# Adding the second-choice rows of four token tiles by DMAs with addition instead of by VectorE

## The reference

```python
logits = xf @ gate_w.T
w, idx = jax.lax.top_k(logits, 2)          # two experts for each of 1024 tokens
w = jax.nn.softmax(w, axis=-1)
combine = zeros((T, 32)).at[arange(T)[:, None], idx].add(w)
out = sum over e of combine[:, e:e+1] * (xf @ expert_w[e].T + expert_b[e])
x = x + out.reshape(x.shape)
```

## Time and profile before

| | us |
|---|---|
| three runs | 287.78, 292.65, 293.7 |
| median | 292.65 |
| the profiled execution's own time | 286.06 |
| its span, first to last instruction | 284.2 |
| mean granted TensorE clock over the span | 0.991 |

### The profile page before, as it was taken

How to read it: one execution, slowest core, us unless ns; L and a number is a source line. 1 busy time by engine, 2 the same in 40 slices (tenths; PEclk the granted TensorE clock), 3 DMA queues, 4 the chain that set the end, 5 groups by cost and what they waited for, 6 DMA issues and landing times.

```text
span 284.2 us, 4478 instructions
## 1 busy us (share of the span) xinstructions
PE 269.6 (95%) x1594; PEld 164.5 (58%) x1594; DVE 140.7 (50%) x404; ACT 77.0 (27%) x138; POOL 69.4 (24%) x69
## 2 busy tenths in 40 slices
PE   7978999999999999999999999999999999999970
PEld 3345677678877778878887775433334333333750
DVE  2368766766913341557441445501665311360895
ACT  1465754334211115223321111221001011113100
POOL 0531600000000000005604113457754442222300
PEclk9999999999999999999999999999999999999996
DMA  7999800000000100019008999926999999984955
GB/s 263 403 352 333 274 12 0 3 0 2 0 37 37 39 1 37 2 44 400 2 4 316 392 421 421 390 76 184 378 405 421 419 413 414 425 361 164 415 198 221
DMA packets 19302, 61.68 MB, mean 217 GB/s; under 512 B 4411, under 2 KB 6107, under 8 KB 14928
## 3 DMA queue, kind: packets, MB, share of 16 engines
q1 hardware_dynamic: 14368, 51.03, 46.2%
q0 software_dynamic: 3472, 7.81, 7.6%
q10 hardware_dynamic: 1440, 2.56, 2.4%
HBM read 54.63 MB, written 13.47 MB: 240 GB/s over the span
## 4 chain that ended last, share of the span: by engine, by line
PE 82%; DVE 8%; DMA 6%; ACT 2%; issue 1%; SPq 0%; DVEq 0%; ACTq 0%; POOLq 0%
PE bank L1368 28%; PE bank L1519 22%; PE bank L1555 15%; DVE acc L1226 4%; PE bank L1492 4%; PE bank L1423 3%; DMA xp_first<-in_xp 2%; PE bank L1251 2%; PE bank L1444 2%; DMA r_tab<-res,recs 2%; DVE acc L1231 2%; DMA wbuf<-r_tab 1%; PE bank L1430 1%; PE bank L1313 1%; DVE y0lo L902 1%
## 5 line engine op out<-in xcount | busy, mean ns | idle before, releaser
L1519 PE MATMUL bank<-wbuf,xT 128*32 128x512 f32 (+1 forms) x432 | 74.0, 598 | 0.0
L1555 PE MATMUL bank<-md,hid 128*128 128x512 f32 x176 | 48.2, 414 | 0.0
L635 POOL DMA_INDIRECT slots<-kept,sid x16 | 15.9, 993 | 122.4 <-DVE sid L1008 119.3
L1519 PEld LDWEIGHTS bank<-wbuf,xT 128*32 128x32 f32 (+1 forms) x432 | 19.9, 122 | 37.5 <-issue 36.5
L1555 PEld LDWEIGHTS bank<-md,hid 128*128 128x128 f32 x176 | 31.7, 189 | 8.3 <-issue 2.9
L1044 DVE COPY xT<-bank 128x512 f32<-128x512 f32 x20 | 13.8, 691 | 44.8 <-PE bank L1492 44.7
L1368 PE MATMUL bank<-y0hi,mg 128*128 128x512 f32 x88 | 35.3, 412 | 0.6 <-ACT y0hi L710 0.6
L1368 PE MATMUL bank<-y0hi,mu 128*128 128x512 f32 x88 | 33.7, 396 | 0.7 <-DVE mu L906 0.7
L1368 PE MATMUL bank<-y0lo,mg 128*128 128x512 f32 x88 | 33.7, 394 | 0.2 <-DVE y0lo L902 0.2
L1368 PE MATMUL bank<-y0lo,mu 128*128 128x512 f32 x88 | 33.6, 393 | 0.0
L828 ACT ACTIVATE res<-bank,recs 128x512 f32<-128x512 f32 x20 | 13.7, 687 | 69.1 <-PE bank L1519 69.1
(11 more groups left out here) (196 smaller groups left out, 300.6 us busy)
## 6 DMA issues: line engine op xcount, KB each, us to landing
wbuf<-in_w SPq DMA_DIRECT2D x32, 1024.0 KB, 13.6
r_tab<-in_zero SPq DMA_DIRECT2D x1, 4096.0 KB, 25.3
wbuf<-r_tab SPq DMA_DIRECT2D x8, 512.0 KB, 7.9
acc<-in_x SPq DMA_DIRECT2D x1, 2048.0 KB, 15.1
y_tab<-yv SPq DMA_DIRECT2D x8, 256.0 KB, 5.7
out<-acc ACTq DMA_DIRECT2D x8, 256.0 KB, 2.2
base<-in_base SPq DMA_DIRECT2D x3, 352.0 KB, 7.3
xp_first<-in_xp SPq DMA_DIRECT2D x1, 1040.0 KB, 7.1
```

The costliest lines, as they stand in the source:

```text
L635: pool.indirect_dma_start(out=slots, out_offset=bass.IndirectOffsetOnAxis(ap=sid[:, j, k:k + 1], axis=0), in_=rec[:, j, k], in_offset=None ...
L1519: v = mm(RS[t % 2][p0:p0 + w], xT[x_slot(t)][:, c, p0:p0 + w], wbuf[buffer(r)][:, c], start=(c == 0), stop=(c == DC - 1))
L1555: v = mm(DN[j % 2][:], hid[:, t, part, c], md[:, c], start=(c == 0 and part == 0), stop=(c == HC - 1 and part == 1))
```

## The change

SyncE now loads both rows only for the tiles 0 to 3, and for the tiles 4 to 7 only the first-choice row. Their second-choice rows are added straight to `acc[:, j]` by four DMAs of 256 KB with `accum_op=ALU.add`, issued by GpSimd at the end of its program, after its own loop and after a semaphore (`rows_out`) that SyncE raises when all scatters have landed. VectorE does one addition instead of two for each of the tiles 4 to 7, and before the first of them it waits until all four accumulating DMAs have landed (`second_in` at 64).

```diff
+        rows_out, second_in = sem("rows_out"), sem("second_in")
@@ block.sync
             for b in range(U):
                 static = len(range(b, TD, U))
                 sp.wait_ge(res_out[b], bodies * 16 + 16 * static if 1 <= b <= XU else 16 * static)
+            sp.sem_inc(rows_out, 1)
             for j in range(NT):
-                sp.dma_start(part(j), r_tab_v[:, 2 * j:2 * j + 2]).then_inc(part_in[j], 16)
+                loaded = 2 if j < TPH else 1
+                sp.dma_start(part(j)[:, 0:loaded], r_tab_v[:, 2 * j:2 * j + loaded]).then_inc(part_in[j], 16)
@@ block.gpsimd, at its end
+            pool.wait_ge(acc2_done, NT)
+            pool.wait_ge(rows_out, 1)
+            for j in range(TPH, NT):
+                pool.dma_start(acc[:, j], r_tab_v[:, 2 * j + 1], accum_op=ALU.add).then_inc(second_in, 16)
@@ block.vector
             def add_part(j):
 
                 dve.wait_ge(part_in[j], 16)
-                for k in range(2):
+                if j >= TPH:
+                    dve.wait_ge(second_in, 16 * TPH)
+                for k in range(2 if j < TPH else 1):
                     link(nc.vector.tensor_tensor(acc[:, j], acc[:, j], part(j)[:, k], ALU.add))
```

## The result

The changed kernel took 295.88 us (median of four runs, 293.88 to 296.52) beside 290.21 us (four runs, 287.45 to 293.7) for the kernel before: a ratio of 1.028 with a 95% interval of 1.019 to 1.036. It is slower; whether by more than 2% this interval leaves open. The ratios leave out slow runs, those more than 1.5% above the fastest of the same kernel, while medians and ranges are of all runs. That matters here: the four runs of the kernel before are two near 287.6 and two near 293.2 us. The ratio of 1.028 fits the means 295.54 and 287.6, a difference of 7.9 us; the medians differ by 5.7 us (1.020), and against the two longer runs it would be some 2.4.

The account below looks back on a forecast made before the run. VectorE's chain of additions was taken to bound the kernel's end; start 267.8, fourth issue 271.8 and landing 3.9 gave T = 275.7, 2.1 us past 273.65, so 294.7 us on the median 292.65, range 288.5 to 298.7.

Parts of the forecast that it names:

- T: Time when the fourth accumulating DMA has landed: GpSimd's start, issues and landing, put at 275.7 us.
- What bounds the kernel: At the end, from 263.96 us, VectorE's unbroken chain of 24 additions; four fewer save 2.9 us at most.
- The end moves with T: VectorE's tail of 7.77 us follows the fourth landing, so the end moves by T - 273.65, +2.1 us.
- small remainder of the pace: Unsized correction in VectorE's chain between the 5.7 us wait less 2.9 saved and the +2.1 us.
- the floor for T: End of VectorE's first eight additions, put at 270.0 us; landing earlier gains no more than 2.9 us.
- rival 2: Descriptor making held up by VectorE's additions, so GpSimd's issues begin only at 270.0: +4.2, 296.9 us; chance 0.06.
- GpSimd's start: First accumulating DMA's issue, 0.5 us behind the third low-part subtraction's end at 267.26: 267.8 us.
- The issues: GpSimd's four direct DMAs, 1.32 us apart like its indirect ones; the fourth issued at 271.8 us.
- The landing: Fourth accumulating DMA, issue to landing: 3.3 us as the gathers plus 0.63 for the second read, 3.9 us.
- Rival 1: At the accumulating DMAs: SyncE-like issues and a 2.7 us landing, T 271.8, end moves -1.9 to 290.8 us; chance 0.12.
- Rival 3: Accumulating DMAs land late, 6.8 us, sharing engines with the loads' rest: T 278.6, +4.9, 297.6 us; chance 0.11.
- Rival 4: DMA engines add much slower than they copy, transfers queue, T = 267.8 + 2.7 + 4x; over 2% from x = 2.25; chance 0.17.

Follow-up runs that it names:

- e2_left_out: The changed kernel without its four GpSimd DMAs and VectorE's wait, second rows of tiles 4 to 7 left out: 283.89 us beside 286.95, ratio 0.989 to the kernel before.
- e12_after: The changed kernel again, unchanged, on another chip, against the kernel before: 290.53 us beside 287.01, ratio 1.011, no stall.
- e11_early: The changed kernel with GpSimd's four DMAs ahead of its third subtraction: 290.13 us, ratio 1.011 to the kernel before.
- e7_one: Only tile 7 gets its second-choice rows by an accumulating DMA, with its own count: 290.46 us beside 291.18 for the kernel before, ratio 0.996.
- e8_after: The changed kernel again, unchanged, on another chip, against the kernel before: 294.1 us beside 291.18, ratio 1.012, with a milder stall.
- e4_before: The kernel before, unchanged, profiled as a control against runs of itself: 286.92 us, ratio 1.001, no stall.
- e6_two: Only tiles 6 and 7 get their second-choice rows by accumulating DMAs, each with its own count: 290.11 us beside 291.18 for the kernel before, ratio 0.993.
- e5_hot_first: The changed kernel with a count per DMA and VectorE's work not touching tiles 4 to 7 of the accumulator first: runs split, 286.82 to 294.37 us.
- e3_each: The changed kernel with a count of its own for each of the four accumulating DMAs: 287.02 us beside 286.95 for the kernel before, ratio 1.000.
- e9_paired: The changed kernel with a count per DMA and each late tile's part and hot sum added together: 285.37 us beside 287.01 for the kernel before, ratio 0.994.

## Why the predicted time was met and the terms behind it were not

**The time: in part luck.** Forecast were +2.1 us on a median of 292.65, 294.7 in all. Measured were 295.88, but beside 290.21 for the kernel before, so +5.7 us. The forecast's time lies within 1.2 us because it started 2.4 us too high. Against the cost without the stall, about 3 us, the forecast of 2.1 is short by 1, and that it isn't short by more is luck too: see T.

**What bounds the kernel: right.** VectorE's chain at the end was the place. Without the second rows (e2_left_out) the time fell by 3.1 us, where 2.9 was worked out.

**The end moves with T: right.** VectorE went idle behind its first eight additions, the accumulating DMA released it, and the tail behind T was 7.77 us in the profile after, as worked out. One row was misread beside it. The addition at 270.02 in the earlier trace rows is the eighth, not the ninth (at 0.73 us of pace the starts from 270.02 to 272.93 are five, the eighth to the twelfth), so the first eight end at 270.7 and the forecast's own T means a wait of 5.0 us, not 5.7. The "small remainder of the pace" is this 0.7 us: 5.0 - 2.9 = 2.1. The time doesn't suffer, as it was worked out from T - 273.65; the floor for T and the start of the issues in rival 2 belong at 270.7 as well.

**T: 1.2 us too early, by three errors that partly cancel.** Counted from VectorE's first part addition, so that executions compare, the prediction put T at 275.7 - 263.96 = 11.7 us, and the execution without the stall had 12.9. The terms:
- GpSimd's start was put 0.5 us behind the subtraction. It was at once (267.29 + 1.74 = 269.03, and the first issue is drawn from 268.97; in other profiles 0.1 to 0.2 us lie between). Counted from VectorE's first addition the start was due at 3.8 us and came at 3.2.
- The issues were put 1.32 us apart, after the indirect DMAs. Direct ones begin 0.58 us apart, also as additions (268.97 to 270.7), nearer to SyncE's price. The fourth was issued 1.7 us behind the first, in place of 4.0: 2.2 us too many.
- The landing was put at 3.9 us and was 7.8. This is the term that was mis-sized most, 4 us too few; the two others take back 2.8 of them, which is luck. The 0.63 us for the second read was put in once, for the last transfer, because issues 1.32 us apart would keep the four from meeting. With issues 0.58 us apart each of the four needs about 1.4 us of the full DMA engines (0.26 MB at 190 GB/s), they queue, and they queue behind the loads as well.

**The rule on reducing transfers.** The Trainium skill, Collectives: The Full Stack, section "The bandwidth ceiling", has a reducing transfer cost double for its two reads. The runs agree, with somewhat more than double: 190 GB/s for additions against 408 for loads in e12_after, and 182 against 393 in the profile after. The error was mine, in charging the doubling to one transfer of four.

**The rivals.** Rival 1's short issues were right, and its early landing was not. Rival 2, the port, can't be seen: GpSimd's four issues took 3.71 us in e11_early, beside VectorE's two-input additions, and 3.72 us in the profile after, where VectorE stood idle for most of them. This agrees with the Trainium skill, SBUF — State Buffer, section "Who interferes with whom". Rival 3's late landing (6.8 us) came near the 7.8, and its cause was half of it: the loads' rest, and the additions' own rate. Rival 4 had the right mechanism, additions queueing in the DMA engines, at 1.4 us each and so short of the 2.25 us from which it makes 2%; its formula with 1.4 us gives T = 267.8 + 2.7 + 5.6 = 276.1.

**The change's cost.** Without the stall it is 1.1%, 3.1 us by that ratio, where 2.1 was forecast. The first comparison's 2.8% holds more. In the profile after, GpSimd's first issue lies 6.5 us behind VectorE's first addition (274.18 - 267.66) in place of the 3.2 of e12_after, because here the loads start 3.1 us behind the issue of the last scatter (260.90 and 263.95) and not 6.3 as in the earlier trace rows. The loads and VectorE are early, while GpSimd's third subtraction waits for TensorE's last tile as it always did. Then the DMA engines fall idle between loads and additions (0 GB/s at 274 us), and GpSimd's place does count: T comes 16.5 us behind the first addition (284.19 - 267.66), not 12.9. With VectorE's 17.45 us from first to last addition in the earlier trace rows as the measure for the kernel before, the cost would be 16.5 + 7.77 - 17.45 = 6.9 us. But that measure is too short for an execution with the stall: two of GpSimd's subtractions then fall beside VectorE's additions, and VectorE's first eight took 7.71 us in the profile after and 6.74 in e12_after, as the first twelve of e7_one took 10.61 and not 9.65. With this 1 us charged to the stall the change costs 5.9 us in the profile after and, worked out in the same way, 3.5 in e8_after. The 10.5 us between the spans of the profiles before and after (284.2 and 294.7) are then 3.7 by which VectorE's first addition comes later, 1.0 of slower additions and 5.9 of the change. By the same sum the kernel before with this stall would take 286.06 + 4.7 = 290.8 us, about what it took on the chip of e8_after (291.18). All this is worked out from single profiles and was not isolated by a run, and it doesn't fit the first chip wholly: there the two longer runs of the kernel before took 292.65 and 293.7 us. How much of the 2.8% is the change stays open.

**What stays open.** The stall near 200 us is not shown to come with the change: it was absent from one profile of the changed kernel (e12_after) and from the seven others taken on its chip and on that of e4_before, and present in those of e8_after, e6_two, e7_one and e5_hot_first on a chip on which the kernel before took longer as well. On the first chip the profile before is without it and the profile after has it. On the other three it went with the chip and not with the kernel. No profile of the kernel before with a stall was taken; that it has the same one rests on its times and mean clocks alone. The DMA engines were full while TensorE stood still (367 GB/s from 200 to 205 us), but so they were in the profile of the kernel before without the stall (371 GB/s). What causes the stall, and whether the changed program has it more often on the first chip, was not found out.

## What to carry to other kernels

Price a transfer with addition at somewhat more than two transfers (190 GB/s against 408 here), and charge it to every byte. Behind 3 MB of loads the four landed when the DMA engines' total work was done, whenever they were issued, as long as the engines didn't run dry in between. An accumulating DMA takes work from a compute engine only where its landing comes before that engine asks for it, so give each its own count (e3_each, worth about 3 us by the ratios), and put what doesn't touch its target ahead of the wait (e9_paired). Measure a short tail from a common event, here VectorE's first addition, since what lies upstream can move by more than the change is worth.

## What the runs showed of the hardware that wasn't expected

- DMAs with addition from HBM into SBUF moved 188 to 193 GB/s with the DMA engines' share at 1.09 to 1.10 (e12_after, 273 to 276 us) and 131 to 197 at 0.97 to 1.09 (the profile after, 277 to 282 us); plain loads in the same executions moved 408 and 393.
- GpSimd's direct DMAs of 128 rows are issued 0.57 to 0.6 us apart, its indirect ones 1.3 us. As copies each is drawn with 0.57 us, as additions with 1.0 for the first and up to 2.0 for the last, at the same pace of issue.
- With loads and additions mixed (e11_early) the DMA engines moved 262 GB/s, and the slowest addition took 11.9 us to land.
- Between the DMA engines' falling quiet and VectorE's resumption more than a us passed: the share was 0.16 in the stretch from 277 us and VectorE resumed at 278.67 (e12_after), 0.05 from 283 us and 284.19 (the profile after).
